# Pairwise maxima with shared middle pairs in the loop's dilation of a fused four-block network on one core

## The reference

```
x = x + _L0_conv_ref(_gn(x))        # 3x3 dilation: max over a window, border -2
x = x + _L1_conv_ref(_gn(x), ...)   # pixel unshuffle, Mamba scan over 4096 tokens, shuffle
x = x + _L2_conv_ref(_gn(x), ...)   # 3x3 convolution, 8 to 8 channels
x = x + _L3_conv_ref(_gn(x), ...)   # 3x3 convolution
```

```
out[y, x] = max_{r, c in 0..2} padded[y + r, x + c]
```

## Time and profile before

| | |
|---|---|
| median of 3 runs | 14411.47 us |
| lowest, highest | 14407.96, 14422.27 us |
| profiled execution: span from first to last instruction | 14402.8 us |
| what lies around the span, against the median | 8.7 us |
| one turn of the loop (image 5 of 0 to 15) | 879.8 us |
| its eight chunks | 113.4, 110.2, 110.2, 110.2, 112.9, 108.9, 105.0, 109.1 us |
| granted TensorE clock, mean | 0.966 |

### The profile page before, as it was taken

The page is one execution under the profiler, slowest core; times in us unless marked ns, Lnnn a source line. Parts: engine busy times, 40 slices in busy tenths (PEclk is TensorE's granted clock), DMA queues, the critical chain, the costliest instruction groups (busy, mean ns, idle before and its releaser), DMA issues.

```text
span 14402.8 us, 165917 instructions
## 1 busy us (share of the span) xinstructions
PE 12558.9 (87%) x28138; PEld 4979.6 (35%) x28138; DVE 13637.5 (95%) x11708; ACT 9660.7 (67%) x18491; POOL 13305.8 (92%) x6039
## 2 busy tenths in 40 slices
PE   5988989888898998989889898898989889899897
PEld 2333333333333333333333333333333333333332
DVE  6999999999999999999999999999999999999995
ACT  5666766666666666666666666676666666666665
POOL 5999999999999999999999999999999999999995
PEclk9999999999999999999999999999999999999999
DMA  3344443434444344443444434444343444434443
GB/s 106 110 124 119 118 124 112 133 109 116 127 114 128 112 117 125 116 127 111 121 122 116 125 110 126 119 118 124 112 132 109 117 126 114 128 112 118 125 116 88
DMA packets 1268462, 1701.57 MB, mean 118 GB/s; under 512 B 403660, under 2 KB 552596, under 8 KB 1267156
## 3 DMA queue, kind: packets, MB, share of 16 engines
q1 hardware_dynamic: 1261572, 1686.16, 40.7%
q10 hardware_dynamic: 5680, 3.15, 0.1%
HBM read 1525.28 MB, written 124.13 MB: 115 GB/s over the span
## 4 chain that ended last, share of the span: by engine, by line
DVE 27%; PE 26%; issue 23%; POOL 12%; DMA 4%; ACT 4%; DVEq 1%; SPq 1%; POOLq 1%; ACTq 0%
DVE h L1368 15%; PE y_ps L1208 15%; POOL hc L709 9%; DVE u_in L1352 8%; PE proj_ps L1149 3%; POOL u_in L683 2%; DMA c_sb<-bc_dram 2%; PE side_ps L1220 2%; DMA raw<-x 2%; PE b_ps L1265 2%; DVE vmax L1331 1%; PE y_ps L1205 1%; ACT a_ps L899 1%; PE side_ps L1194 1%; PE side_ps L1224 1%
## 5 line engine op out<-in xcount | busy, mean ns | idle before, releaser
L709 POOL TENSOR_TENSOR hc<-h,c_sb 128x1024 f32<-128x1024 f32 x4096 | 9607.9, 2367 | 815.5 <-DVE h L1368 703.9
L1368 DVE TENSOR_TENSOR_SCAN h<-a_ps,carry,u_in 128x512 f32<-128x512 f32 x7168 | 8757.6, 1263 | 193.4 <-POOL hc L709 114.3
L1208 PE MATMUL y_ps<-hc,ident 128*128 128x512 f32 x16400 | 8070.1, 617 | 427.4 <-POOL hc L709 420.6
L899 ACT ACTIVATE a_ps<-dt,a_neg 128x512 f32<-128x512 f32 x8192 | 5567.5, 687 | 4121.8 <-DVE h L1368 4069.2
L1208 PEld LDWEIGHTS y_ps<-hc,ident 128*128 128x128 f32 x16400 | 3119.1, 196 | 4031.1 <-issue 2975.8
L1352 DVE TENSOR_TENSOR u_in<-dtx,b_ps 128x1024 f32<-128x1024 f32 x2816 | 3362.9, 1194 | 76.5 <-PE b_ps L1265 44.5
L683 POOL TENSOR_TENSOR u_in<-dtx,b_sb 128x1024 f32<-128x1024 f32 x1280 | 3029.4, 2367 | 0.0
L1265 PE MATMUL b_ps<-b_parts,select 96*128 96x512 bf16 x2816 | 1115.8, 396 | 1039.6 <-DVE u_in L1352 1037.0
L1368 DVE TENSOR_TENSOR_SCAN h<-a_ps,u_in 128x512 f32<-128x512 f32 x1024 | 1200.6, 1208 | 238.8 <-ACT a_ps L899 194.5
L1265 PEld LDWEIGHTS b_ps<-b_parts,select 96*128 96x128 bf16 x2816 | 282.1, 100 | 2540.2 <-DVE u_in L1352 1988.8
L1149 PE MATMUL proj_ps<-u_ln,w_x 128*128 128x512 f32 x2064 | 972.2, 593 | 4.6 <-ACT u_ln L851 3.7
(11 more groups left out here) (129 smaller groups left out, 7438.9 us busy)
## 6 DMA issues: line engine op xcount, KB each, us to landing
c_sb<-bc_dram SPq DMA_DIRECT2D x4100, 256.0 KB, 3.2
b_sb<-bc_dram SPq DMA_DIRECT2D x1282, 256.0 KB, 3.2
z<-x_dram SPq DMA_DIRECT2D x68, 512.0 KB, 8.5
x_dram<-vmax SPq DMA_DIRECT2D x66, 512.0 KB, 4.6
raw<-x SPq DMA_DIRECT2D x129, 256.0 KB
x_dram<-x SPq DMA_DIRECT2D x129, 256.0 KB, 3.8
out<-raw SPq DMA_DIRECT2D x256, 128.0 KB
x<-x_dram SPq DMA_DIRECT2D x128, 224.0 KB, 7.4
```

Source lines behind the costliest of these rows:

```text
L709: pool.tensor_tensor(hc[:, ring_at(c * S + s, HC_RING)], h[:, ring_at(c * S + s, H_RING)], c_sb[:, s // C_GROUP % C_RING, s % C_GROUP:s % ...
L899: act.activation(a_ps[:, a_slot(c * S + s, half)], dt[:, c % 2, half], ACT.Exp, scale=a_neg[:, at:at + 1]).then_inc(a_made, 1)
L1208: mm = pe.matmul(y_ps[:, half], ident[:, :], hc[:, ring_at((c * S + s) % (NC * S), HC_RING), half], start=False, stop=(s == S - 1), skip_g ...
L1368: dve.tensor_tensor_scan(h[:, r, half], a_ps[:, a_slot(c * S + s, half)], u_in[:, s % U_RING, half], start, ALU.mult, ALU.add).then_inc(h_ ...
```

## The change

The loop's dilation takes pairs. Of the rows 0 to 5 of a band (four rows and one on each side), the pairs (1, 2) and (3, 4) are each in two of the four windows of three. So per direction VectorE makes

1. the two pairs' maxima (512 elements), in place in `side_ps`,
2. the windows that end the pair with the row before it (512 elements),
3. the windows that end it with the row behind it (512 elements),

and the same over columns, with 128 pairs in each of four rows. These are six TENSOR_TENSOR of 512 elements a band in the slots 9, 10, 11 and 13, 14, 15, where four TENSOR_REDUCE stood in 9, 11, 13, 15. In each of them one operand is in PSUM and one in SBUF. The operand in PSUM is put there by ScalarE (`copy_middles`): in slot 8 the normalised odd rows from `raw` (two pointer operands, 512 elements, contiguous rows), in slot 12 every second column of `vmax` (512 elements, in steps of 8 bytes). VectorE's reads and two of its writes over columns go in steps of 8 bytes too. `side_ps` gets two more uses a band, ("peak", k, 0) and ("peak", k, 1), each a pair of semaphore steps; the first row of `PLACES` moves from (15, 16, 18, 19, 22) to (18, 19, 20, 21, 22), so that a convolution piece starts behind them. `vmax` is used one column further right. `dilate_first` is as it was. The number of steps that `dil` counts in a band stays the same.

```diff
-PLACES = ((15, 16, 18, 19, 22), (24, 25, 26, 27, 28), (29, 30, 31, S + 1, S + 2))
+PLACES = ((18, 19, 20, 21, 22), (24, 25, 26, 27, 28), (29, 30, 31, S + 1, S + 2))
-DIL_SLOTS, ADD_DILATED, DILATED_OUT, STORE_ROWS = (6, 9, 11, 13, 15), ((26, 27), (29, 30)), (26, 29), 31
+NORM_BAND, MIDDLES, PEAKS, PEAK_AT = 6, (8, 12), ((9, 10, 11), (13, 14, 15)), (9, 13)
+ADD_DILATED, DILATED_OUT, STORE_ROWS = ((26, 27), (29, 30)), (26, 29), 31
...
+            at_state["peak", c - 1, half] = (PEAK_AT[half],)
...
+            def copy_middles(number, k, way):
+
+                act.wait_ge(side_emptied, used(number - 1, "peak", k, way))
+                if way == 0:
+                    normed(RAW, side_ps[:, :].rearrange("p (r w) -> p r w", w=W),
+                           raw[:, k * R + 1:k * R + 4:2, :]).then_inc(side_filled, 1)
+                else:
+                    act.wait_ge(dil, number * DIL + 5 + 6 * k + (k > 0) + (k in (0, BANDS - 1)) + 2)
+                    act.activation(side_ps[:, :].rearrange("p (r w) -> p r w", w=W // 2), vmax[:, :, 1:W:2],
+                                   ACT.Copy).then_inc(side_filled, 1)
...
+                    pe.wait_ge(side_emptied, read(number - 1, "peak", k, 1))
...
+            def dilate(number, k, way, step):
+
+                at = number * DIL + 5 + 6 * k + (k > 0) + (k in (0, BANDS - 1)) + 2 * way
+                use = ("peak", k, way)
+                if way == 0:
+                    odd, even, first, last = (side_ps[:, :].rearrange("p (r w) -> p r w", w=W), norm[:, 2:5:2, 1:W + 1],
+                                              norm[:, 0:3:2, 1:W + 1], norm[:, 3:6:2, 1:W + 1])
+                    to_first, to_last = vmax[:, 0:R:2, 1:W + 1], vmax[:, 1:R:2, 1:W + 1]
+                else:
+                    odd, even, first, last = (side_ps[:, :].rearrange("p (r w) -> p r w", w=W // 2), vmax[:, :, 2:W + 1:2],
+                                              vmax[:, :, 0:W:2], vmax[:, :, 3:W + 2:2])
+                    to_first, to_last = norm[:, 1:R + 1, 1:W:2], norm[:, 1:R + 1, 2:W + 1:2]
+                if step == 0:
+                    dve.wait_ge(dil, at)
+                    dve.wait_ge(side_filled, used(number - 1, *use))
+                    dve.tensor_tensor(odd, odd, even, ALU.max).then_inc(dil, 1)
+                elif step == 1:
+                    dve.wait_ge(dil, at + 1)
+                    if k and way == 0:
+
+                        dve.wait_ge(x1_rows_out, number * (BANDS * 16) + k * 16)
+                    dve.tensor_tensor(to_first, odd, first, ALU.max).then_inc(dil, 1)
+                else:
+                    dve.tensor_tensor(to_last, odd, last, ALU.max).then_inc(side_emptied, 1)
```

More of the change, by code:

```diff
@@ L478, in store_x1_rows @@
                 sp.dma_start(x1_dram.rearrange("c (g l) r q w -> l (c g) r (q w)", l=BANDS)[k],
-                             (vmaxs[k % 2] if number is None else vmax)[:, :, 0:W]
+                             (vmaxs[k % 2] if number is None else vmax)[:, :, 1:W + 1]
                              ).then_inc(first_rows_out[k] if number is None else x1_rows_out, 16)
@@ L669, in add_band @@
             def add_band(norm, vmax, k):
-                return pool.tensor_tensor(vmax[:, :, 0:W].rearrange("p r (q w) -> p r q w", q=R),
+                return pool.tensor_tensor(vmax[:, :, 1:W + 1].rearrange("p r (q w) -> p r q w", q=R),
                                           norm[:, 1:R + 1, 1:W + 1].rearrange("p r (w q) -> p r q w", q=R),
@@ L941, in copy_dilated @@
                 rows = slice(half * R // 2, (half + 1) * R // 2)
-                out = act.activation(vmax[:, rows, 0:W].rearrange("p r (q w) -> p r q w", q=R),
+                out = act.activation(vmax[:, rows, 1:W + 1].rearrange("p r (q w) -> p r q w", q=R),
                                      proj_ps[:, :].rearrange("p (r w q) -> p r q w", q=R, r=R // 2), ACT.Copy)
@@ L1079, in _ @@
                                 pad(b, n, part)
-                        if 1 <= c <= BANDS and s == DIL_SLOTS[0]:
+                        if 1 <= c <= BANDS and s == NORM_BAND:
                             normalise_band(b + 1, c - 1)
+                        if 1 <= c <= BANDS and s in MIDDLES:
+                            copy_middles(b + 1, c - 1, MIDDLES.index(s))
                         if 1 <= c <= BANDS and s in DILATED_OUT:
@@ L1233, in extra @@
                 name, *at = use
+                if name == "peak":
+                    return
                 if name in ("conv", "conv_last"):
@@ L1315, in convolution_weights @@
                                 own(dve.tensor_tensor(w_main[n][:, dw, :], w_main[n][:, dw, :], cen[:, 0:P], ALU.add))
-            def dilate(number, k, step):
-                at = 4 + 6 * k + (k > 0) + (k in (0, BANDS - 1)) + step + 1
-                dve.wait_ge(dil, number * DIL + at - 1)
-                row = R // 2 * ((step - 1) % 2)
-                if k and step == 1:
-                    dve.wait_ge(x1_rows_out, number * (BANDS * 16) + k * 16)
-                max_of_3(norm[:, :, :], vmax[:, :, :], row, step).then_inc(dil, 1)
+            def dilate(number, k, way, step):
[20 more added lines that the diff above has]
+                    dve.tensor_tensor(to_last, odd, last, ALU.max).then_inc(side_emptied, 1)
             def max_of_3(norm, vmax, row, step):
@@ L1413, in _ @@
                             split_lo(b, c)
-                        if 1 <= c <= BANDS and s in DIL_SLOTS[1:]:
-                            dilate(b + 1, c - 1, DIL_SLOTS.index(s))
+                        for way in range(2):
+                            if 1 <= c <= BANDS and s in PEAKS[way]:
+                                dilate(b + 1, c - 1, way, PEAKS[way].index(s))
             gate(B, 0)
```

## The result

The change makes the kernel faster: 14212.44 us median of 4 runs (14207.4 to 14224.48) against 14411.88 (4 runs, 14407.96 to 14422.27) for the kernel before, a ratio of 0.9862 with the 95% interval 0.9848 to 0.9876. The profiled execution has a span of 14205.1 us and a time of 14207.4; the median is 7.3 us above the span, where 8.7 was taken over from before.

What follows compares the result with a forecast made beforehand. VectorE alone was taken to set the pace in chunks 1 to 4, about 5 us above a floor shared with GpSimd. 14402.8 - 220 + 2 + 24 = 14209 us of span, 8.7 more give 14217; range 14185 to 14320.

Steps and rivals of the forecast that it cites:

- Four reductions for six maxima: VectorE, banded chunks: four reductions at 6.92 us replaced by six maxima at 3.48, 64 bands, -220 us.
- rival B: VectorE's column maxima: steps of 8 bytes cost double, 1.6 us a band, 102 us, 14319 us; chance 0.07.
- the bound that I set by it: Upper price of the three column maxima: twice per element, 1.6 us a band more; none was taken.
- The wait in slot 28: VectorE waits 0.37 us for TensorE's broadcast, 0.55 us later through the moved z product; 64 bands, +24 us.
- rival C: TensorE becomes the bound: none of its idle 1.17 us usable, VectorE waits 1.54 us, 75 us more, 14292; chance 0.13.
- that idle time: TensorE's idle 1.14 us before slot 21's broadcast, forecast to shrink to about 0.9.
- ScalarE's copies: Two copies a band, slots 8 and 12, hidden except 0.1 us in chunk 4, 16 times: +2 us.
- just in time: Chunk 4, slot 8: the copy would end at 5048.7, when VectorE's first maximum can start at 5048.76.
- GpSimd nothing: GpSimd has 6.4 us free in chunk 2 and keeps 2.9; no cost taken.
- Rival D: GpSimd's burst around slots 22 to 26: chunk 6's 1.1 us wait in each of 64, 70 us, 14287; chance 0.11.
- rival E: TensorE's clock stays low past slot 16: VectorE waits about 12 us a band, 770 us, 14960 us; chance 0.05.
- Chunks 5 and 7 nothing: Convolution pieces move there too; costed at nothing, or 1 us each (32 us in all) without idle cover.

Runs made afterwards that it cites:

- z's product earlier: The changed kernel with the convolution product that adds z in slot 20 instead of 21, ahead of slot 21's broadcast: 14174.98 us, ratio 0.9841.
- rows by pairs only: The changed kernel with pairs over rows only; columns keep two reductions in slots 13 and 15, without the second copy: 14313.29 us, ratio 0.9939.
- the move alone: The kernel before with only the convolution piece's new slots (18, 19, 20, 21, 22), no maximum changed: 14429.64 us, ratio 1.0016.
- the windows in one besides: The changed kernel with both a pair's windows in one operation and the product adding z in slot 20: 14163.28 us, ratio 0.9829.
- the windows in one: The changed kernel with both windows of a pair made by one operation of 1024 elements: 14188.17 us, ratio 0.9848; one profiled execution took 26480.51.

## Why the prediction was right, point by point

14217 us was forecast with a range of 14185 to 14320, and 14212.44 measured; faster by over 0.2% had 0.91. The forecast's span, 14209, stands to a measured 14205.1.

- **Four reductions for six maxima, 3.44 us a band, -220 us.** The step of 0.58 us was right in all six (0.582 to 0.585 from start to start in the mean), and with z's product earlier chunk 2 falls by the full 3.4 us. The choice to count steps and not lengths was the right one, though the two were 10 us apart. In the Trainium skill (VectorE: DVE Perf Modes) the section that I cited also sends its reader on to "Two Vector instructions with no wait between them", by which an operation that isn't held starts earlier; the starts here, 0.1 us ahead of the end of a 0.67 us record, agree with that.
- **Steps of 8 bytes (rival B).** 663 to 674 ns with and without them. The rival is out, and the bound that I set by it was never near.
- **The wait in slot 28, 0.37 us, +24 us.** Measured 0.35 to 0.37 us in chunks 1 to 4, 23 us in 64 bands. The whole of TensorE's idle time behind slot 21 could be used, so rival C is out. The rule that gave it, that work put behind a broadcast is paid from the idle pieces between it and the next broadcast that VectorE waits for, also gave the way out: the idle time ahead of slot 21 was there to be had. One number on the way was wrong: that idle time was to shrink to 0.9 us and measured 1.76, with another 1.23 for a product of GpSimd's in front of it. The sum didn't use it, so the 0.37 is untouched. But a product that needs 1.72 us would not have fitted into 0.9, so the way out could not be read from the prediction's own number.
- **ScalarE's copies, +2 us.** 0.75 us for a bound of 0.80, and 0.63 where 0.58 was taken, with no wait for either in any chunk. The 0.58 came from a copy out of PSUM; a copy into it is a little longer. My +2 didn't appear, but "just in time" was right: in chunk 4 the smallest room is 0.08 us.
- **GpSimd nothing.** 103.63 us busy in chunk 2 against 103.78 before, and no wait of the scan for `hc` in the banded chunks. Rival D is out.
- **TensorE's clock (rival E).** The idle time ahead of slot 15's broadcast was to shrink by 0.2 us and fell from 4.52 to 2.96. Before, the granted clock drops to 0.5 in chunk 2 of all 15 images; after, in 7 of them, and image 5, with 1.00, is one of the others. Chunk 2 is 107.2 to 107.3 us long either way. Nothing of the sort that I feared in slots 16 to 21 is there. The run with rows by pairs only shows that the mechanism is real on a small scale: there the clock fell behind slot 21's broadcast in 13 of 60 chunks, at 1.65 us each.
- **Chunks 5 and 7 nothing.** Right as a sum, but not looked at closely enough: chunk 5 came out 0.87 us shorter. It scatters by several us from image to image, in before as in after, and what its 14 us are made of was not settled; the move alone has 10 of them. In image 5 its waits have other names after (before, then after):

```profile
DVE h L1368 <- POOL hc L709: 3.8, 2, 2.0
DVE u_in L1352 <- PE b_ps L1265: 0.8, 2, 0.5
```

```profile
DVE h L1401 <- ACT a_ps L901: 1.9, 2, 1.4
DVE u_in L1385 <- PE b_ps L1283: 1.5, 1, 1.5
```

- **Chunk 4 was missed.** It gave 2.63 us and not 3.07. Most of the difference is a wait of VectorE for the row of state 7 in `b_ps` (in its slot 6), 2.16 us in the mean over 16 images before, 2.58 after, 2.69 with the move alone, 2.16 with z's product earlier. No term of the sum had it. What it consists of is under the last heading: it comes in two sizes, and the mean only counts them.

The span came out 4 us below the sum. Behind that stand misses that cancel: the banded chunks gave 184 us where 196 were forecast (7 of the 12 in chunk 4, and 5 in chunks 2 and 3, which fell by 2.9 us each and not 3.07), and chunk 5 gave 14 where nothing was. The two large terms, the six for four (3.39 us a band for 3.44) and the wait of slot 28, are each within about 3 us.

## What to carry to other kernels

On an engine that sets the pace, count an instruction by the distance to the next start, and a reduction over overlapping windows by what it reads: for the same 1024 maxima over three rows, two reductions cost 3.64 us and three pairwise maxima that share the middle pair 1.75. When work is pushed to a later slot on another engine, look for the idle piece that it will be paid from, and on which side of the next awaited broadcast it lies: one slot was worth 37 us here, 23 of them the wait itself. And a second operand in PSUM is worth a copy where GpSimd works in SBUF all the time: without it, what an operation waits depends on where it starts in GpSimd's product, here from 0.15 us to two products of 2.37.

## What the runs showed of the hardware that I had not expected

**The same idle time, and two clocks.** In chunk 4 TensorE waits 1.96 us for ScalarE's statistics, `few`, and then computes two products into `side_ps` (L1210, four records), behind which the broadcast stands that VectorE wants. Two images of the kernel after, from TensorE's timeline:

```profile
4954.68 1.98 PE L1210 MATMUL side_ps<-zs,w_out 128*128 128x512 f32 x4 [1.96 <-ACT few L749]
...
8429.16 3.48 PE L1210 MATMUL side_ps<-zs,w_out 128*128 128x512 f32 x4 [1.96 <-ACT few L749]
```

and the windows of the two stretches, slots 4 and 5:

```profile
4951.42:4957.25 5.83, 3.88 (x10) 1.48 (x9) 5.83 (x6) 4.99 (x14) 5.83 (x4) 1.00 0.31 91
8425.91:8431.74 5.83, 3.87 (x8) 1.35 (x7) 5.83 (x6) 4.99 (x14) 5.83 (x4) 0.81 0.26 91
```

Everything ahead is alike to a hundredth: the same idle 1.96 us, the same work. In the one image the clock stays at full, in the other it is 0.81 over the window, the two products take 1.5 us longer, and VectorE waits 3.5 us instead of 1.8. The chunk grows by 1.35 us, 109.90 to 111.25, as a wait of 0.65 us for a decay in slot 9 gives way to one of 0.29 for `b_ps`. Which it will be changes from image to image: 3 of 16 images have the long form before, 7 after, 8 with the move alone, 3 with z's product earlier, 5 with the windows in one besides, and none with rows by pairs only, though the idle time is 1.95 to 1.96 us in every one of them. At 1.35 us each, the four images between 3 and 7 are 5 us, most of the 0.44 us of chunk 4 above. Whether the change makes the long form more likely or these are chance, the runs don't settle; the same goes for some 5 of the 37 us by which z's product earlier beats the change.

**An execution at a clock below both levels.** The long execution of the windows in one, by its row of clocks on the page and by two windows:

```profile
PEclk8999999999999999311111111111111111112222
```

```profile
1000.00:6000.00 5000.00, 4442.13 (x10061) 1768.07 (x10059) 4816.31 (x4200) 3481.65 (x6648) 4776.41 (x2168) 0.98 0.42 122
13000.00:26000.00 13000.00, 13000.00 (x5684) 4170.77 (x5683) 2771.72 (x2373) 1978.52 (x3741) 2720.12 (x1228) 0.18 0.09 26
```

For the first 16 of 40 slices it ran like the others, at 0.98. Then the granted clock fell to 0.16, below both 2.4 and 1.2 GHz, for 13.3 ms, and was at 0.26 in the last 2.5 (0.18 in the mean of the second window): TensorE is busy without a break, and the others wait for it. Eight other executions of the same kernel, four beside it and four later, took 14182 to 14197 us. What lowered the clock isn't in the trace. A single time that is far off belongs beside its row of clocks before anything is read from it.
